# A mixture of experts behind three attentions: the last tags go out earlier, the table is turned earlier, and the row gathers stand in one row

## What is computed

```python
logits = jnp.einsum('btc,ec->bte', x, router_w)
top_vals, top_idx = jax.lax.top_k(logits, TOP_K)        # 2 of 16 experts
gates = jax.nn.sigmoid(top_vals)
...
h = jax.nn.silu(gate) * up                              # per expert, 256 wide
out_all = jnp.einsum('neh,ehc->nec', h, down_w)
moe = jnp.einsum('ne,nec->nc', w_full, out_all)
...
shared = jnp.einsum('bts,cs->btc', jax.nn.silu(sg) * su, shared_down_w)
return moe + shared
```

## Time and profile before

| | |
|---|---|
| median of 3 runs | 1397.54 us (1389.95 to 1399.03) |
| profiled execution | 1392.92 us |
| its span, first to last instruction | 1391.2 us |
| PE busy | 1263.2 us (91%) |
| DVE busy | 872.5 us (63%) |
| ACT busy | 708.1 us (51%) |
| POOL busy | 523.9 us (38%) |
| moved by DMA | 131.58 MB, 95 GB/s over the span |

### The profile page before, as it was taken

One profiled execution on the slowest core, in us unless ns is written; L12 is line 12 of the kernel. 1 busy time (PEld: TensorE's weight loads), 2 busy tenths in 40 slices (PEclk: granted clock), 3 DMA queues, 4 the chain that ended last, 5 costly groups with the idle time before them and its releaser, 6 DMA issues. The chain is left out here.

```text
span 1391.2 us, 19205 instructions
## 1 busy us (share of the span) xinstructions
PE 1263.2 (91%) x6164; PEld 613.7 (44%) x6164; DVE 872.5 (63%) x1998; ACT 708.1 (51%) x1290; POOL 523.9 (38%) x731
## 2 busy tenths in 40 slices
PE   6899989989999999999999999998899888999996
PEld 3232332323243224453453444443242344679885
DVE  5888789788877886458557567468767413222221
ACT  2345445556645655546546556456656541136553
POOL 4444251154312411327217217225413122356665
PEclk9698999999999999999999999999999989999999
DMA  8573422314431333033123123124522003943341
GB/s 245 145 240 84 128 78 77 108 61 124 136 120 24 107 92 103 5 107 107 47 62 107 46 61 107 46 62 122 137 84 47 17 16 88 342 112 54 55 56 21
DMA packets 113219, 131.58 MB, mean 95 GB/s; under 512 B 17017, under 2 KB 93305, under 8 KB 112867
## 3 DMA queue, kind: packets, MB, share of 16 engines
q1 hardware_dynamic: 102867, 119.91, 29.5%
q0 software_dynamic: 10256, 10.45, 4.5%
HBM read 83.25 MB, written 48.40 MB: 95 GB/s over the span
## 5 line engine op out<-in xcount | busy, mean ns | idle before, releaser
L1288 DVE TENSOR_REDUCE Mx<-bank 128x1 f32<-128x512 f32 x512 | 339.1, 685 | 206.8 <-PE bank L1022 203.6
L904 ACT ACTIVATE prob<-bank 128x512 f32<-128x512 f32 x576 | 332.1, 594 | 262.4 <-PE bank L1048 253.0
L1048 PE MATMUL bank<-QS,KS 99*128 99x512 bf16 x768 | 297.1, 388 | 39.4 <-ACT prob L904 20.1
L1022 PE MATMUL bank<-KS,QS 96*128 96x512 bf16 x768 | 298.7, 390 | 13.9 <-DVE Mx L1285 7.2
L1061 PE MATMUL bank<-prob,V 128*17 128x512 f32 x1536 | 207.5, 613 | 1.7 <-issue 1.7
L904 ACT ACTIVATE prob<-prob 128x512 f32<-128x512 f32 x192 | 120.9, 630 | 159.9 <-DVE prob L1299 159.0
L1048 PEld LDWEIGHTS bank<-QS,KS 99*128 99x128 bf16 x768 | 75.0, 98 | 234.6 <-ACT prob L904 125.7
L1022 PEld LDWEIGHTS bank<-KS,QS 96*128 96x128 bf16 x768 | 76.3, 99 | 125.2 <-issue 48.5
L1285 DVE CUSTOM_DVE_ANT_0 bank<-bank,ff_h 128x512 f32<-128x512 f32 x128 | 87.9, 696 | 22.2 <-PE bank L1022 21.7
L741 POOL TENSOR_SCALAR parts<-rest 128x512 bf16<-128x512 f32 x47 | 29.1, 619 | 185.8 <-DVE rest L1248 185.2
L727 POOL TENSOR_SCALAR shift<-mv 128x4 f32<-128x4 f32 x28 | 5.5, 196 | 239.2 <-DVE mv L1209 239.2
(11 more groups left out here) (178 smaller groups left out, 1863.1 us busy)
## 6 DMA issues: line engine op xcount, KB each, us to landing
stack_scr<-parts SPq DMA_DIRECT2D x48, 384.0 KB, 2.6
QS<-stack_scr SPq DMA_DIRECT2D x47, 384.0 KB, 4.2
KS<-stack_scr SPq DMA_DIRECT2D x47, 384.0 KB, 5.1
stack_scr<-parts SPq DMA_DIRECT2D x48, 256.0 KB, 2.9
w_gu<-in_gate_up SPq DMA_DIRECT2D x16, 512.0 KB
stack_scr<-parts SPq DMA_DIRECT2D x48, 128.0 KB, 2.8
cT<-in_ctxT SPq DMA_DIRECT2D x8, 512.0 KB, 5.7
w_dn<-in_down SPq DMA_DIRECT2D x16, 256.0 KB
```

The costliest lines, as they stand in the source:

```text
L904: act.activation(prob[:, u % NP_, j, :], src, ACT.Exp, scale=CAST).then_inc(exp_done, 1)
L1022: pe.matmul(m, QS[0:STACK, h, qt * P:(qt + 1) * P], KS[0:STACK, h, :], start=True, stop=True).then_inc(s_full, 1)
L1048: pe.matmul(bankT[e % NT][:, :], KS[0:ROWS, h, kt * P:(kt + 1) * P], QS[0:ROWS, h, :], start=not on_pe, stop=True).then_inc(t_full, 1)
L1288: dve.tensor_reduce(dst, b, AX.X, ALU.max).then_inc(s_read, 1)
```

## The change

There are four parts.

1. The last batch dispatches in the first program too, at its step r + 1.25; the second program no longer writes tags.
2. `turn_table` and `addresses` move from behind block (1, 1) to behind block (0, 2) of the shared stage, and no longer wait for `y_read`. SP waits for the table (`table_in`) before it issues the first weight.
3. All 47 gathers stand in a row ahead of sum 0, with no gather among the sums. `xr` grows from 28 to 33 places, and the other 14 are in memory that is free by then: `hT_last[0]` and `hT_last[1]`, four places each, and the shared gate and up weights `s_gu`. For these 14 (four, four and six) the gather waits until PE has read the old contents (`up_full`). The waits for `y_read` and `sg_done` are gone, and the one for the gather eight before stays; the first four gathers are counted on the `sum_out` semaphores.
4. The landing counts start 16 higher, for those four, and SP's branch `s <= NY` is gone: sums 1 to 4 wait by the same rule as all others.

```diff
@@ batch_order
-            if n < NB - 1:
-                for t in range(QT):
-                    place(r + 2 + t, ("dispatch", p, t))
-            else:
+            for t in range(QT):
+                place(r + 2 + t if n < NB - 1 else r + 1.25, ("dispatch", p, t))
+            if n == NB - 1:
@@ experts
-        NX = 28
+        NX = 33
+        TURNED_AT = (0, 2)
...
+        spare = [h.rearrange("p k (a n) -> p (k a) n", n=D) for h in hT_last[0:2]]
+        spare.append(s_gu.rearrange("p i k (a n) -> p (i k a) n", n=D))
+        homes = [xr[:, i, :] for i in range(NX)] + [h[:, i, :] for h in spare for i in range(h.shape[1])]
+        homes_free = NX * [0] + 4 * [HT] + 4 * [2 * HT] + 8 * [3 * HT]
...
-        after_sum = {8 + i: n_last - QT + 1 + i for i in range(QT)}
-        after_gate = {13 + 2 * i: LATE * HT - HT + 2 + i for i in range(HT - 1)}
-        after_sum.update({20 + i: n_last + 1 + i for i in range(QT)})
+        def rows_landed(s):
+
+            if s < NY:
+                return sum_out[s], 16
+            return xr_in[(s - NY) % ROWS_SEM], 16 * ((s - NY) // ROWS_SEM + 1)
@@ SyncE
+                sp.wait_ge(table_in, 16)
                 for n in range(NE):
...
-                    last = sum_out[(s - 1) % NY]
-                    if s <= NY:
-                        sp.wait_ge(last, 16)
-                    else:
-                        sp.wait_ge(last, sp.value_load(landings[0:1, s:s + 1], min_val=16, max_val=8 * TILES))
+                    sp.wait_ge(sum_out[(s - 1) % NY],
+                               sp.value_load(landings[0:1, s:s + 1], min_val=16, max_val=8 * TILES))
                     sp.sem_inc(apart, 1)
@@ GpSimd
-                pool.iota(landed[0:1, 1:TILES + 2], [[16, (TILES + 1) // NY], [0, NY]], base=0, channel_multiplier=0,
+                pool.iota(landed[0:1, 1:TILES + 2], [[16, (TILES + 1) // NY], [0, NY]], base=16, channel_multiplier=0,
...
-                for t in range(TT - QT, TT):
-                    for k in range(2):
-                        pool.indirect_dma_start(tag_scr, bass.IndirectOffsetOnAxis(slot[:, t, k:k + 1], 0),
-                                                tags[:, t, k, :], None).then_inc(tagged, 16)
...
-                for s in range(NX):
-                    if s in after_sum:
-                        pool.wait_ge(y_read, after_sum[s])
-                    if s in after_gate:
-                        pool.wait_ge(sg_done, after_gate[s])
+                    landed_on, count = rows_landed(s)
+                    if count > 16:
+                        pool.wait_ge(landed_on, count - 16)
+                    if homes_free[s]:
+                        pool.wait_ge(up_full, homes_free[s])
...
+                for s in range(TILES):
                     rows(s)
                 pool.wait_ge(rows_out, 16 * B)
...
-                    if s % 2 == 0 and NX + s // 2 < TILES:
-                        rows(NX + s // 2)
@@ TensorE and VectorE, shared stage
-                        if c == 1 and m == 1:
+                        if (c, m) == TURNED_AT:
                             turn_table()
...
-                    pe.wait_ge(y_read, QT)
```

More of the change, by code:

```diff
@@ L1627, in _ @@
                         if n >= NY:
[L1628 removed]
+                            act.wait_ge(sum_out[n % NY], 16 + 16 * (n // NY))
                         act.activation(yt[:, n % NY, :], bank[4 + n % 4][:, 0:D], ACT.Identity,
@@ L1639, in down_products @@
                             pe.wait_ge(y_read, n - 3)
-                        if n == 2 * QT - 1:
+                        if n == QT - 1:
                             pe.wait_ge(token_ready, 1)
@@ L1674, in turn_rows @@
                     for k in range(KD):
-                        ins = pe.transpose(bank[s % 2][:, k * P:(k + 1) * P], xr[:, s % NX, k * P:(k + 1) * P],
+                        ins = pe.transpose(bank[s % 2][:, k * P:(k + 1) * P], homes[s][:, k * P:(k + 1) * P],
                                            identf[:, :])
```

14 lines of the change are left out of this document (4 added, 10 removed).

## The result

The first measurement gave 1411.24 us (median of 4, 1409.19 to 1415.83) against 1396.89 for the kernel before (median of 4, 1389.95 to 1399.03): a ratio of 1.014, interval 1.011 to 1.017. The forecast was 1386.8, so it was wrong by 24 us and in sign. The same kernel was measured again on three numbered chips. On two of them (0 and 14) it is faster than before, by about what the sum said, and on the third (8) it is slower again. Both findings have to be explained.

A forecast was written before the change was run, and what follows sets the result against it. The tile stage's chain of waits, led by landings of scattered sums, was taken as the bound, not arithmetic or bytes alone. Gains of 6.8 + 3.96 = 10.7 us off 1397.5 gave 1386.8 us, range 1378 to 1394.

The forecast's parts named there:

- 47 gathers in a row: POOL before sum 0: a 1.25 us pace, 58.75 us in all, 1182.9 to 1241.7; sum 0 still at 1243.00.
- Rival 2: Tile stage: if ScalarE's 2.44 us idle before its third sgt goes, 12.3 us gained, 1385.2; chance 0.14.
- Rival 4: SyncE's first wait: queues at 227 GB/s shared with gathers, weights late, tiles start 47 us late, 1434; chance 0.04.
- The term: Shared-stage expert weights: 12.58 MB from 1177, 10 us at 354 GB/s then 265, ending 1221, margin 7 to 12 us.
- Sums 1 to 3: Tile stage: these sums stop waiting for landings, so sum 9 starts at 1267.8 instead of 1274.57, 6.8 us gained.
- The three bare gathers behind S9: POOL after sum 9 starts: gathers standing bare before sums 13, 21 and 37 go, 3 x 1.32 = 3.96 us gained.
- The span's end: End of the tile stage: 10.7 us earlier, at 1380.5, or 210.5 us after the second program's start.
- Rival 1: Tile stage: landings take back what the gathers leave, 1390.7, or 1389.6 if sums 1 to 3 still wait; chance 0.18.
- Rival 3: Gather stream before sum 0: slow, sum 0 late; all gain lost at a 1.62 us pace, 1401 at 1.7; chance 0.04.
- Tags, table, token: First program and shared stage: eight tag DMAs free, 3.2 us cover; table lands 1177, token 1182.6, 17 us earlier.

The follow-up runs named there:

- the version with waits: The changed kernel with the y_read and sg_done waits back before gathers 8 to 27: 1389.06 us on chip 13, 1405.74 us (ratio 1.0098) on chip 7.
- the tags-only version: The kernel before with only the last batch's eight tag stores moved into the first program: 1381.11 us against 1382.14, ratio 0.9991.
- the version with sums 1 to 3 alone: The kernel before with only the landing waits of sums 1 to 3 removed (branch gone, counts 16 higher): 1376.98 us, ratio 0.9963.
- four variants without a stall: Chip 13, once each: changed kernel with progress waits back 1389.06, without SyncE's table wait 1369.77, gathers behind weights 1404.22; kernel before without progress waits 1382.53 us.

## Why the prediction was wrong, and where it was right

**The step that failed** is "47 gathers in a row", and in it the half sentence "The waits for y_read and sg_done go". I priced what the waits cost POOL, and asked nothing of what they did for the others. They stood in front of eleven gathers (not thirteen, as I wrote ahead of the prediction) and kept them to eight in a row, then to one or two, and twice to five. Without them 37 stand in a row (47 where nothing stalls), and on some chips TensorE's results then reach ScalarE and VectorE 4 to 34 us late: 34.1 us in the first measurement, 31.2 on chip 8. The changed kernel had it in the profiled run of the first measurement and of chip 8, and all 8 runs of the two lie between 1409.19 and 1415.83; on chips 0 and 14 its 14 runs lie between 1366.57 and 1376.35. That the row is the condition rests on three comparisons of the kernels: before and after on chip 8 (1395.74 against 1411.79); the weights' wait taken out, which leaves the stall; and the version with waits, where a signal is 0.9 us late in the paced stretch and ScalarE waits 17.07 us in the unpaced one. It isn't shown on one and the same chip by that edit alone, since the changed kernel was measured on chip 8 and the version with waits on 7. Why it happens on some chips, and by what mechanism, stays open.

**The trace of before had the warning**, in the first program, where I had not looked. POOL stores the tags of the earlier batches there in rows of indirect DMAs, 1.3 us apart. ScalarE's `prob` (the attention's exponential) comes late beside two of them, a row of six from 1052.45 and a row of eight from 1113.28:

```profile
1061.07 0.60 ACT L904 ACTIVATE prob<-bank 128x512 f32<-128x512 f32 x1 [2.88 <-remote]
...
1123.20 0.60 ACT L904 ACTIVATE prob<-bank 128x512 f32<-128x512 f32 x1 [1.72 <-PE bank L1048]
```

The changed kernel on chip 0, at the place of the second one (its row starts at 1106.24):

```profile
1115.16 0.60 ACT L903 ACTIVATE prob<-bank 128x512 f32<-128x512 f32 x1 [0.71 <-PE bank L1047]
```

All 20 traces divide in this way. In the five of the first measurement and of chips 7 and 8, kernel before included, this wait is 1.70 to 1.74 us beside the row of eight and at longest 1.49 to 2.88 us beside the row of six. In the 15 of chips 0, 13 and 14 it is 0.71 and 0.93 us. The late signal comes when the row ends: at most 0.1 us ahead of the end of its last store and at most 1.3 us behind it. ScalarE's signal behind the 37 gathers came 1.8 us ahead of the row's end to 4.6 us behind it. So in these traces the delay goes with the length of the row: up to 2 us beside six or eight, 31 to 34 beside 37. Not every short row does it. Nothing is late in before beside the first eight gathers, nor beside the eight tag stores that it has in its second program.

Before's second program has late signals too, towards the end of its gathers, and the forecast was built on them:

```profile
1241.60 0.47 ACT L1629 ACTIVATE yt<-ebank,gate 128x256 f32<-128x256 f32 x1 [1.66 <-remote]
```

This is yt0 at 71.61, where the tags-only version on chip 14 has it at 69.84. The third sgt of the earlier trace rows follows with 2.44 us of idle, against 0.82 there.

**The clue that I passed over:** the range was built on the medians' spread and on waits that the profile names. Rival 2 named a signal that came late with its matmuls long done, and took it only for time that might be won. None of my rivals had it growing.

**Rival 4, on the slower side,** had the right place (the shared stage beside the late weights, first product after 1234.3) and the wrong mechanism. The weights landed at 58.4 us on chip 0 and were needed at 63.1, a margin of 4.7 where I had 7 to 12; they were forecast for 51. The term was mis-sized: 12.58 MB took 49.8 us from the first DMA, 253 GB/s on average, and not 354 and then 265, since with token as early as 12.7 the gathers share the queue almost from the start (the q1 queue carried 5.22 MB in 20 us of it, 261 GB/s). The Trainium skill's rule that DMAs of all issuers share the same 16 engines ("DMA: Bandwidth & Descriptors", section "Issuing engines are not separate DMA queues") is what these windows show, 364 to 369 GB/s for both together. With the weights 20 us later this rival's mechanism is real, and costs 26 us of first product (90.15 against 64.25).

**The sum was right in size** wherever no signal was late. Its terms need a base without late signals, which is the tags-only version on chip 14:
- Sums 1 to 3: forecast 6.8 at S9. Alone (chip 0) they bring 5.2 (103.29 less 98.14), in the whole 6.3 (103.29 less 96.97, chip 14).
- The three bare gathers behind S9: forecast 3.96, so 105.2 us from S9 to S46. The changed kernel took 104.3 to 105.1 us in three traces, the tags-only version 110.0 and the kernel before 109.17: 4.0 to 5.7.
- The span's end: forecast 210.5, measured 210.06, 209.89 and 209.18. On chip 14 that is 11.3 us ahead of the tags-only version (220.44 less 209.18), forecast 10.7.
- The time: 8.3, 9.6 and 11.4 us less than before in three measurements, forecast 10.7.

Rival 1 is out: no landing took the gathers' place. Of rival 2 the first half came true where no signal was late: on chip 0 yt3 starts at 78.44 and yt9 at 95.66, 1.6 us ahead of what the forecast took, and S9 at 96.95, 0.85 ahead. But the tags-only version has yt3 at 78.45 as well, so this is the chip's doing and no gain of the change. Rival 3 is out too: the gathers kept their 1.25 us even in the stall, and took 0.94 to 0.99 us also beside DVE's 0.69 us operations.

**Tags, table, token:** cost nothing, as forecast (ratio 0.9991 alone). The table's gather came at 3.40 and the first row gather at 12.73, forecast 2.3 to 3.3 and 12.9; the table turned without a wait with SyncE's wait in place, and 1.1 to 1.4 us late without it.

**The first program's 7.0 us** are no effect of the change. On chips 0, 13 and 14 the second program starts between 1157.03 and 1163.23 in variants with and without the tags. Of the 5.4 us between the changed kernel's first trace and its trace on chip 0, 4.9 arise between 1116 and 1131, instruction by instruction. They begin at the late `prob` beside the row of eight tag stores, 1.0 us late at 1116.23. TensorE, which waits for it, stands 1.68 us instead of 0.69, and then the granted clock falls. The other 3.9 us come with the low clock (the third column from the right), 0.57 in the first trace and 1.00 in the other:

```profile
1120.00:1130.00 10.00, 8.67 (x26) 6.86 (x27) 1.49 (x4) 2.48 (x3) 0.00 (x0) 0.57 0.00 0
```

```profile
1120.00:1130.00 10.00, 9.26 (x31) 5.62 (x30) 3.86 (x11) 3.39 (x6) 1.68 (x4) 1.00 0.00 0
```

The trace of before has the same: against the version with sums 1 to 3 alone on chip 0 it loses 2.0 us at the row of six and 4.9 at and behind the row of eight. So the kernel before pays for such rows too.

A version that is faster than before on every chip wasn't found by a run. The one with sums 1 to 3 alone is the candidate: it keeps the waits between the gathers and was 4.1 us faster on chip 0, and was not run on chips 7 and 8.

## What to carry to other kernels

A wait that paces a stream of indirect DMAs may be there for the engines beside it; before it is taken away, ask what the stream does unbroken, and for how long. Look in the trace of before for shorter rows of the same kind, in every stage: a waiting engine whose releaser had finished 1 to 2 us earlier was the sign here. A blind sum can be right term by term and still have the wrong sign, if the stall lies where the change adds no instruction. Run the changed kernel itself again beside its variants before a cause is read out of them: four variants without a stall meant nothing, since on that chip the changed kernel very likely had none either (the waits beside the tag stores are short there, 0.71 and 0.93 us).

## What I had not expected of the hardware

- The same program, beside the same 366 GB/s and the same pace of gathers, stalls 31 to 34 us in one stage on some chips and not at all on others: 1411.24 and 1411.79 us against 1370.77 to 1372.78. Chips 7 and 8, and that of the first measurement, also run the kernel before more slowly: 1390.47, 1395.74 and 1396.89 against 1381.1 to 1385.89. Part of that is the late signals beside its own rows of tag stores and what follows them, 2.0 and 4.9 us in the trace of before.
- These chips' traces lack landing events, of the weights 381 of 512 in the first measurement and 389 on chip 8, but also 103 in the kernel before, which has only short late signals; the other chips' traces have them all, or all but one. Whether the lost events and the late signals have one cause, and whether the recording takes part in it, stays open: every time here comes with the records of its run, and there was no run without.
- In rows that follow a pause, the first late signal was due 6.7 to 10.5 us into the row, six to nine DMAs: in the rows of six and eight tag stores at 6.7 and 8.9 us, and in the rows of gathers at 1186.2 where it began at 1175.71 and at 1191.4 on chip 8 where it began at 1180.95. On chip 7, where the row of 24 gathers from 1234.16 follows others after 0.7 to 1.5 us of pause, ScalarE's sgt is 1.0 us late at 1237.68 already. There TensorE itself also hesitates, its matmuls 0.4 to 1.0 us apart. Whether TensorE's results, its increments or their delivery are late, the trace doesn't tell.
